# A transformer block with routed experts on one core: order of the drain, and smaller sums on VectorE

## The reference

```python
h = layernorm(x) * (1 + ca) + sa
x = x + ga * attention(h)              # 16 heads of 8, rotary, causal
h = layernorm(x) * (1 + cb) + sb
xn = h * rsqrt(mean(h * h) + eps) * ln_w
vals, idx = top_k(xn @ Wg + bg, 2)     # 2 of 8 experts
w = softmax(vals)
x = x + gb * sum_k w_k * (silu(xn @ W1a_e + b1a_e) * (xn @ W1b_e + b1b_e) @ W2_e + b2_e)
```

## Time and profile before

| | |
|---|---|
| median of 3 runs | 554.0 us |
| profiled execution | 553.08 us, span 551.0 us |
| granted TensorE clock, mean | 0.94 |
| busy: TensorE, VectorE, ScalarE, GpSimd | 450.4, 438.3, 369.2, 329.2 us |
| instructions | 20,072 |

### The profile page before, as it was taken

One profiled execution on the slowest core, in us unless ns is written; L12 is line 12 of the kernel. 1 busy time (PEld: TensorE's weight loads), 2 busy tenths in 40 slices (PEclk: granted clock), 3 DMA queues, 4 the chain that ended last, 5 costly groups with the idle time before them and its releaser, 6 DMA issues.

```text
span 551.0 us, 20072 instructions
## 1 busy us (share of the span) xinstructions
PE 450.4 (82%) x6425; PEld 327.7 (59%) x6426; DVE 438.3 (80%) x1397; ACT 369.2 (67%) x913; POOL 329.2 (60%) x472
## 2 busy tenths in 40 slices
PE   4688999988889888988889787987599999999300
PEld 2445566655556555655555676976487878888300
DVE  4478888999999999998998488778467777777467
ACT  2346778777676776777765667767578888988400
POOL 3433356577777778777765458866334544555554
PEclk9999999998999999998997789889889999999955
DMA  8411011122022211222001301224621111111086
GB/s 222 123 29 42 23 41 51 56 65 67 11 70 71 66 50 28 70 70 65 31 25 51 84 26 56 61 70 96 157 60 49 53 55 49 51 53 38 14 263 195
DMA packets 44891, 37.95 MB, mean 69 GB/s; under 512 B 9235, under 2 KB 37478, under 8 KB 44801
## 3 DMA queue, kind: packets, MB, share of 16 engines
q1 hardware_dynamic: 35328, 25.59, 18.1%
q0 software_dynamic: 4544, 8.54, 4.4%
q10 hardware_dynamic: 4928, 2.67, 1.6%
HBM read 24.77 MB, written 12.78 MB: 68 GB/s over the span
## 4 chain that ended last, share of the span: by engine, by line
DVE 36%; PE 21%; issue 14%; ACT 10%; DMA 7%; SPq 6%; POOL 3%; DVEq 1%; ACTq 1%; POOLq 0%
DVE nmax L848 8%; DVE qk_tok L1142 4%; DVE xhat L816 3%; PE bank L1247 3%; ACT silu_a L755 3%; DVE hl L1129 3%; ACT qk_t L721 2%; DVE send L930 2%; PE bank L1254 2%; DMA out_dram<-we_lo 2%; PE bank L1289 2%; POOL expert_outs L607 2%; PE bank L1267 2%; ACT qk_tok L745 2%; DVE turn_s L832 2%
## 5 line engine op out<-in xcount | busy, mean ns | idle before, releaser
L848 DVE TENSOR_REDUCE nmax<-bank 128x2 f16<-128x384 f32 (+1 forms) x192 | 114.8, 600 | 20.9 <-PE bank L1254 19.0
L662 ACT ACTIVATE probs<-bank 128x512 f32<-128x512 f32 (+1 forms) x192 | 100.4, 524 | 42.1 <-PE bank L1279 41.3
L607 POOL DMA_INDIRECT expert_outs<-qk_tok,number_of x78 | 79.0, 1012 | 75.9 <-ACT qk_tok L745 56.8
L1142 DVE SCALAR_TENSOR_TENSOR qk_tok<-bank,b_sb,silu_a 128x256 f32<-128x256 f32 x156 | 72.5, 480 | 50.9 <-ACT silu_a L755 49.6
L1247 PE MATMUL bank<-qk_t 24*64 24x64 f16 (+3 forms) x1024 | 74.5, 246 | 27.7 <-DVE nmax L848 18.4
L1442 PE MATMUL bank<-xt,we_hi 128*128 128x256 f16 x312 | 87.0, 279 | 3.4 <-DVE qk_tok L1142 2.3
L1444 PE MATMUL bank<-xt,we_lo 128*128 128x256 f16 x312 | 86.9, 279 | 0.0
L1443 PE MATMUL bank<-xt,we_hi 128*128 128x256 f16 x312 | 86.7, 278 | 0.0
L736 ACT ACTIVATE hh<-qk_tok 128x256 f16<-128x256 f32 x156 | 64.4, 413 | 26.5 <-DVE qk_tok L1142 25.3
L510 POOL DMA_INDIRECT expert_rows<-send,pos_i x64 | 64.9, 1013 | 27.1 <-DVE tok L935 15.2
L755 ACT ACTIVATE silu_a<-bank,b_sb 128x256 f32<-128x256 f32 x156 | 69.1, 465 | 13.7 <-PE bank L1444 12.7
(11 more groups left out here) (165 smaller groups left out, 1087.7 us busy)
## 6 DMA issues: line engine op xcount, KB each, us to landing
g_in<-expert_rows SPq DMA_DIRECT2D x39, 132.0 KB
qk_t<-nmax_t SPq DMA_DIRECT2D x256, 0.5 KB
mod_b<-mod_rows SPq DMA_DIRECT2D x16, 256.0 KB
we_lo<-expert_outs SPq DMA_DIRECT2D x16, 256.0 KB, 3.5
wstage<-in_L_ffn_W1a_dram SPq DMA_DIRECT2D x16, 128.0 KB
wstage<-in_L_ffn_W1b_dram SPq DMA_DIRECT2D x16, 128.0 KB
wstage<-in_L_ffn_W_dram SPq DMA_DIRECT2D x16, 128.0 KB
out_dram<-we_lo ACTq DMA_DIRECT2D x16, 128.0 KB, 3.8
```

Of the source, the lines that this page charges most:

```text
L607: pool.indirect_dma_start(out=outs, out_offset=bass.IndirectOffsetOnAxis(ap=number_of[:, r, s:s + 1], axis=0), in_=y_sb[:, r, s, :], in_of ...
L662: nc.scalar.activation(probs[:, k // 3, first:end], col_bank[k % 2][:, 0:end - first], ACT.Exp, scale=SM_SCALE).then_inc(probs_ready, 1)
L848: nc.vector.tensor_reduce(nmax[:, pair, js[0]:js[-1] + 1, 3 * DK + c], scores, AX.X, ALU.max, negate=True).then_inc(max_ready, 1)
L1142: nc.vector.scalar_tensor_tensor(out=h32[:, f], in0=banks[f][:, TS:2 * TS], scalar=b1_sb[:, 1, bass.ds(e * FB + f, 1)], in1=silu_a[:, f], ...
```

## The change

It does five things. The drain's order: the first table is made at step 0 of iteration 15, the loads of tiles 0 to 3 go ahead of that iteration's `mod_b` load, ranks and places move from step 10 to step 11 in the drain, the last table begins one step earlier (its first step at the end of iteration 18), and the dummy rows are written in iteration 19 ahead of the loads of tiles 13 and 14. Token numbers come from a constant plus 4 times the batch, without the running counter. The comparison with the chosen indices reads the integers, without the cast. Both norms' variances are taken in one instruction at step 4, and raised to the power in one. The two sums take the same tensor as a second input, by a maximum that changes nothing.

```diff
                 if s2:
...
                     sp.dma_start(mod_b[:, i % 2, :], ...)
                 if s1:
                     place_max(i + 1, 1)
-                if i == B - 1:
-                    sp.wait_ge(early_table.sem, len(early_table.names))
...
-                    for n in range(4):
-                        load(tile_number(n))
+                if i == B + 3:
+                    sp.wait_ge(last_table.sem, last_table.after(0, "ends"))
+                    pad_experts()
                 if i >= B:
-                    n = 3 * (i - B) + 3
-                    for n in range(max(n, 4), n + 3):
+                    n = 3 * (i - B) + 4
+                    for n in range(n, min(n + 3, EARLY)):
                         load(tile_number(n))
```

```diff
-                if norm:
-                    pool.wait_ge(vecn.sem, vecn.after(bn, "var"))
-                    nc.gpsimd.tensor_tensor(rstd0[:], ve0[:], power, ALU.pow).then_inc(pooln.sem, 1)
-                if routing:
-                    par = bb % 2
-                    pool.wait_ge(vec3b.sem, vec3b.after(bb, "var"))
-                    nc.gpsimd.tensor_tensor(rstd3[:], ve3[:], power, ALU.pow).then_inc(pool3b.sem, 1)
+                if norm or routing:
+                    norms = norms_of(norm, routing)
+                    pool.wait_ge(var_ready, i + 4)
+                    nc.gpsimd.tensor_tensor(rstd[:, norms], ve[:, norms], power[:, norms], ALU.pow).then_inc(rstd_ready, 1)
```

```diff
-                nc.vector.tensor_scalar(ve[:], mv[:, :, 1], EPS_LN, None, ALU.add).then_inc(vecs.sem, 1)
+                nc.vector.scalar_tensor_tensor(out=ve[:, norms], in0=mv[:, norms, :, 1], scalar=EPS_LN, in1=mv[:, norms, :, 1], op0=ALU.add, op1=ALU.max).then_inc(var_ready, 1)
...
-                    nc.vector.tensor_copy(top_f[:], top_i[:, :, 0:K]).then_inc(vec3c.sem, 1)
-                    vec.wait_ge(vec3c.sem, vec3c.after(b, "idxf"))
...
-                                            top_f[:].unsqueeze(3).broadcast_to([P, NS, K, E]), ALU.is_equal).then_inc(vec3c.sem, 1)
+                                            top_i[:, :, 0:K].unsqueeze(3).broadcast_to([P, NS, K, E]), ALU.is_equal).then_inc(vec3c.sem, 1)
...
-                    nc.vector.tensor_copy(to_send[:, :, :, W_IDX].bitcast(I32), tok[:]).then_inc(vec_place.sem, 1)
+                    nc.vector.scalar_tensor_tensor(out=to_send[:, :, :, W_IDX].bitcast(I32), in0=tok, scalar=float(NS * K * b), in1=tok, op0=ALU.add, op1=ALU.max).then_inc(vec_place.sem, 1)
...
-                    nc.vector.tensor_scalar(tok[:], tok[:], float(NS * K), None, ALU.add).then_inc(vec_place.sem, 1)
...
-                        if k == 10:
+                        if k == (10 if i < B else 11):
                             place(bs)
...
-                    if i == B - 1 and k == 3:
+                    if i == B - 1 and k == 0:
                         first_tiles()
+                    if i == B + 2 and k == NK - 1:
+                        last_tiles(0)
                     if i == B + 3:
-                        last_tiles(k)
+                        last_tiles(k + 1)
...
-                    if placing and k == 10:
+                    if placing and k == (10 if i < B else 11):
                         pe.wait_ge(logits_ready, bs + 1)
                         ranks(bs)
```

More of the change, by code:

```diff
@@ L271, in build @@
         pe3b = steps("pe3b", "xn_t logits")
-        vec3b = steps("vec3b", "stats0 stats1 aggr0 aggr1 var xhat0 xhat1 ms")
+        vec3b = steps("vec3b", "stats0 stats1 aggr0 aggr1 xhat0 xhat1 ms")
         vec_xn = steps("vec_xn", "xn0 xn1")
         logits_ready = sem("logits_ready")
-        vec3c = steps("vec3c", "max0 max1 idx0 idx1 idxf chosen member gap")
+        vec3c = steps("vec3c", "max0 max1 idx0 idx1 chosen member gap")
         act3b = steps("act3b", "sq0 sq1")
@@ L306, in pipeline, with norms_of @@
                 iteration(i, *(0 <= i + n < B for n in (-4, -3, -2, -1, 0, 1, 2, 3)))
+        def norms_of(norm, routing):
+            return slice(0 if norm else 1, 2 if routing else 1)
         def pair_of(b, half):
@@ L415, in iteration @@
                     sp.dma_start(wstage[:, par, 2, :].rearrange("p (c d) -> p c d", d=D), w2_v[b // 2, par]).then_inc(wstage_in[par], 16)
+                if i == B - 1:
+                    sp.wait_ge(early_table.sem, len(early_table.names))
+                    sp.wait_ge(sent[0], 64 * ((EARLY_B + 1) // 2))
+                    sp.wait_ge(sent[1], 64 * (EARLY_B // 2))
+                    for n in range(4):
+                        load(tile_number(n))
                 if s2:
@@ L502, in _ @@
             pool.wait_ge(init_vec, 2)
-            power = c32[:, C_POW:C_POW + NS]
+            power = c32[:, C_POW:C_POW + 2 * NS].rearrange("p (n s) -> p n s", s=NS)
             def send_rows(b, n):
@@ L807, in moments, with variance, normed @@
                     nc.vector.bn_aggr(mv[:, s], st[:, s]).then_inc(vecs.sem, 1)
-            def variance(b, vecs, mv, ve):
-                vec.wait_ge(vecs.sem, vecs.after(b, "aggr1"))
-                nc.vector.tensor_scalar(ve[:], mv[:, :, 1], EPS_LN, None, ALU.add).then_inc(vecs.sem, 1)
-            def normed(b, vecs, pools, mv, rstd, xhat):
-                vec.wait_ge(pools.sem, pools.after(b, "rstd"))
+            def variance(i, norm, routing):
+                norms = norms_of(norm, routing)
+                if norm:
+                    vec.wait_ge(vecn.sem, vecn.after(i + 3, "aggr1"))
+                if routing:
+                    vec.wait_ge(vec3b.sem, vec3b.after(i - 2, "aggr1"))
+                nc.vector.scalar_tensor_tensor(out=ve[:, norms], in0=mv[:, norms, :, 1], scalar=EPS_LN, in1=mv[:, norms, :, 1], op0=ALU.add, op1=ALU.max).then_inc(var_ready, 1)
+            def normed(i, b, vecs, mv, rstd, xhat):
+                vec.wait_ge(rstd_ready, i + 4)
                 for s in range(NS):
@@ L962, in iteration @@
                         if k == 3:
-                            moments(bn, vecn, st0, mv0)
-                            variance(bn, vecn, mv0, ve0)
+                            moments(bn, vecn, st0, mv[:, 0])
                         if k == 8:
-                            normed(bn, vecn, pooln, mv0, rstd0, xhat0)
+                            normed(i, bn, vecn, mv[:, 0], rstd[:, 0], xhat0)
                     if routing:
@@ L973, in iteration @@
                         if k == 4:
-                            moments(bb, vec3b, st3, mv3)
-                            variance(bb, vec3b, mv3, ve3)
+                            moments(bb, vec3b, st3, mv[:, 1])
                         if k == 6:
-                            normed(bb, vec3b, pool3b, mv3, rstd3, xhat3)
+                            normed(i, bb, vec3b, mv[:, 1], rstd[:, 1], xhat3)
                         if k == 10:
                             mean_square(bb)
+                    if (norm or routing) and k == 4:
+                        variance(i, norm, routing)
                     if s0:
```

28 lines of the change are left out of this document (10 added, 18 removed).

## The result

The changed kernel took 538.0 us (median of 4 runs, 537.1 to 541.0) against 554.4 for the kernel before: a ratio of 0.972 with a 95% interval of 0.968 to 0.976. Measured a second time it was 536.0 against 555.1, ratio 0.966 (0.963 to 0.969). So it is 16 to 19 us faster. As a gain, 21.5 us were forecast and, by the ratios, 15.6 and 18.9 came. The profiled execution took 537.12 us with a span of 535.0 us and a mean granted clock of 0.957.

What follows compares the result with a forecast made beforehand. VectorE's list was taken to bound the steady iterations. Attention 9.1, first table 1.0, ranks 3.3 and dummy writes 8.1 sum to 21.5 us, giving 532.5 us against the median; range 521 to 545, the forecast's own 527 to 538.

Steps and rivals of the forecast that it cites:

- Bound and mechanism: Steady attention iterations: VectorE's list is the loop; four savings shorten it by 0.91 us in ten iterations, 9.1 us.
- Index cast: Attention on VectorE: removing the cast L899 saves 0.19 us an iteration, the comparison on integers taken as unchanged.
- Two-input form of L930: Token numbers on VectorE: the new form still waits for GpSimd's L524, so 0 of a possible 12.7 us.
- the rival at 524.5 us: Two-input forms run beside GpSimd, so some 8 of L930's 12.7 us go as well; chance 0.15.
- One variance: Attention's norms: first variance gone, 0.19 us an iteration; second starts ahead of GpSimd's L535, no longer held, 0.45 us.
- the counter L935: Token counter on VectorE in attention: its removal saves 0.08 us an iteration, between 0 and 0.16.
- First table: Iteration 15: table before the gate ends the wait for first rows but stalls TensorE some 3 us; 1.0 us gained.
- Ranks: Drain: ranks one step later save VectorE's idle 1.1 us at three iteration heads, 3.3 us, between 0 and 7.5.
- Dummy rows: Drain: earlier dummy writes remove 6.0 us of standing at tile 15 and 2.1 of slow clock, 8.1 us.
- Slower by a held product: Rival: the product L922 is held in each of 12 iterations, 2.1 us each, giving 558 us; chance 0.05.

Runs made afterwards that it cites:

- e10: The changed kernel with the cast of the chosen experts' indices put back ahead of the comparison: 540.7 us, ratio 0.974.
- e5: The changed kernel with the variance and the token numbers as one-input instructions in place of the two-input forms: 537.8 us, ratio 0.968.
- e7: The changed kernel with all batches' token numbers worked out in the set-up and written by a reduction over one element: 537.4 us, ratio 0.962.
- e9: The changed kernel with two variances and two powers again in place of the merged ones: 541.9 us, ratio 0.972.
- e2: The kernel before with only the drain's ranks and the placement's first matrix product moved from step 10 to 11: 553.7 us, ratio 0.999.
- e1: The kernel before with only the dummy rows written earlier, behind the last table, and that step's loads starting one later: 547.6 us, ratio 0.989.
- e3: The kernel before with only the first table at step 0 and the first expert loads ahead of mod_b: 554.2 us, ratio 1.001.

## Why the prediction was right, point by point

- **Bound and mechanism.** Right. VectorE's list was the loop of the steady iterations; shortening it by 0.91 us was forecast, 0.80 came (17.41 to 16.61). That attention alone took 9.6 us (7.5 to 11.6) off the time, for 9.1, is in part luck: the forecast counted ten iterations, eight had the gain, and from the fourth to the last L524 the traces show 7 us, of which some 0.7 are an interval behind a low clock that no longer occurs. What makes up the rest was not located.
- **Index cast, 0.19 us.** Right: 0.20 (e10). The comparison on integers costs little: 0.18 us in the steady iteration, where it was 0.20, and over all sixteen a mean of 249 ns where it was 203.
- **Two-input form of L930: nothing.** Right, and the rival at 524.5 us was wrong twice: the form is held as before (e5), and where it is not (e7), the hold moves on and 0.2 us an iteration are left of 1.4, not the greater part.
- **One variance: 0.19 + 0.45.** The size was wrong and part of the mechanism: merging is worth 0.33 (e9). The variance is indeed ahead of L535, by 0.12 us where 0.16 was forecast, but it is so with two variances as well. GpSimd's shorter power, which I counted at nothing, is the largest thing that merging saves, by way of the scalings that it lets go sooner. Of the 0.80 us, 0.20 are the cast's, 0.33 merging's, and 0.27 are left for the counter L935 and the hold that went; these two were not separated.
- **First table: 1.0 gained.** Not seen: -0.3 us (-2.0 to 1.3). The wait for the first rows went, 2.2 us, and the stall at the gate came, 1.6 to 1.8 us for some 3 forecast.
- **Ranks: 3.3.** This step failed most. I priced it by VectorE's idle time at the head of the next iterations; alone it gave 0.7 us (-1.1 to 2.4). The waits for the gap went, and waits for the sums grew from 3.1 to 8.7 us in e2: what TensorE no longer waits for the gap it waits for the sums. VectorE's idle time at the heads went, but 3.2 us of it came back further on, for the residual sum and for silu. Within the whole change the part's worth is open, with 0.6 and 3.8 us as the two estimates.
- **Dummy rows: 8.1.** The stall of 6.0 went as forecast and the loads of tiles 13 and 14 stayed early. The slow clock behind it was mis-sized: 7.3 us in each of nine traces, 6.0 of them by the sum of tile 13 and 1.3 by the next, so 1.3 and not 2.1.
- **Slower by a held product.** Did not come: L922 takes no more than 0.35 us in any trace with the changed attention. Nor does it in e1, e2 and e3: the wait that this rival built on was one of the profiled execution.

By the values above, the time where there is one and the trace for the dummy rows, the terms were too large by 2.6 us (ranks), 1.3 (table) and 0.8 (dummy rows), and attention's too small by 0.5: 4.2 us together. The gain fell short of its 21.5 us by 5.9 in the first measurement and by 2.6 in the second. By the times of the four parts alone, 16.0 us, it would be 5.5. Each single measurement carries some 2 us either way.

## What to carry to other kernels

Price a wait by what is late next on the engine that ends it: a wait that only changes its name (here from the gap to the sums) is worth little, and a gain ahead of a stall that another event ends goes into the stall. When a held instruction is made free, look at the two behind it before counting the hold as gained, and when the holding engine's list gets shorter, look at what it holds next. And before a difference of 1 or 2 us between two traces is read as the change's, look for it in a third trace whose code is the same there.

## What the runs showed of the hardware

- In the changed kernel the granted clock reads 1.00 from 40 to 46 us, though the products there take 661 ns; in e2, where they take 660, it reads 0.50, the lower of the two levels (1.2 of 2.4 GHz). Of the ten traces in which these products take 660 or 661 ns, seven read 1.00 there and three 0.50. Here the durations tell the level, and the clock's column does not.

```profile
40.00:46.00 6.00, 5.39 (x58) 2.86 (x56) 2.83 (x10) 2.99 (x6) 0.33 (x1) 1.00 0.01 3
```
```profile
40.00:46.00 6.00, 5.39 (x50) 2.61 (x45) 3.00 (x10) 2.75 (x5) 0.70 (x1) 0.50 0.01 3
```

- A power over 4 elements a partition takes GpSimd 1.04 us and two of them over 2 elements take 1.38. By an estimate from these two sizes, 0.34 us of each belong to the instruction and 0.18 to each of its elements.
